# FFN weight tiles of an attention and FFN kernel: transposed by DMA from SBUF instead of by TensorE

## The reference

```
x = x + Wo(softmax(q k^T) v),  q from layernorm(x), k and v from the context
x = x + FFN(layernorm(x))
FFN: gate = q_act(x) @ q_w(w_gate)^T;  up = q_act(x) @ q_w(w_up)^T
     out  = q_act(silu(gate) * up) @ q_w(w_down)^T
q_w: blocks of 32 share a power-of-two scale; elements are rounded and clipped to +-6 times it
```

## Time and profile before

| | |
|---|---|
| median of 3 runs | 2190.7 us (2190.6 to 2194.46) |
| the profiled execution | 2190.88 us |
| its span, first to last instruction | 2189.3 us |
| outside the span | 1.6 us |
| PE / DVE / ACT / POOL busy | 95% / 70% / 47% / 36% |
| mean granted TensorE clock | 0.986 of full |

### The profile page before, as it was taken

The page is one execution under the profiler, slowest core; times in us unless marked ns, Lnnn a source line. Parts: engine busy times, 40 slices in busy tenths (PEclk is TensorE's granted clock), DMA queues, the critical chain, the costliest instruction groups (busy, mean ns, idle before and its releaser), DMA issues.

```text
span 2189.3 us, 49860 instructions
## 1 busy us (share of the span) xinstructions
PE 2085.6 (95%) x15818; PEld 1535.8 (70%) x15818; DVE 1533.2 (70%) x3455; ACT 1035.8 (47%) x2760; POOL 791.9 (36%) x1093
## 2 busy tenths in 40 slices
PE   6899999999999999999999999999999978999996
PEld 5678777877787877777787877787888853444442
DVE  6777776777777776777676767676665548777774
ACT  7755554555555554545454545455544532333331
POOL 4333333332333333333232323331111006666664
PEclk9999999999999999999999999999999998999998
DMA  6733433232333333333333333232232253544444
GB/s 219 185 79 73 83 69 88 64 78 69 79 73 78 74 76 76 76 76 76 72 76 76 76 76 76 67 74 62 61 63 59 52 152 65 85 82 84 84 84 66
DMA packets 398607, 179.55 MB, mean 82 GB/s; under 512 B 361984, under 2 KB 374784, under 8 KB 398400
## 3 DMA queue, kind: packets, MB, share of 16 engines
q1 hardware_dynamic: 375616, 125.10, 27.7%
q0 software_dynamic: 16608, 45.36, 8.5%
q10 hardware_dynamic: 6176, 6.29, 0.9%
HBM read 61.08 MB, written 27.26 MB: 40 GB/s over the span
## 4 chain that ended last, share of the span: by engine, by line
PE 80%; issue 4%; DVE 4%; DMA 4%; POOL 3%; ACT 3%; SPq 1%; POOLq 0%; DVEq 0%; ACTq 0%
PE b_qk L1019 30%; PE b_v L1019 15%; PE b_o L1074 7%; PE b_c L1019 7%; PE b_s L1019 7%; PE b_w L1074 7%; DMA attn_weights<-x_scratch 2%; POOL attn_weights L514 2%; PE b_pt L1019 1%; DMA probT<-psplit 1%; PE b_x L1019 1%; PE b_w L1162 1%; PE b_x L1026 1%; DVE inner_amax L951 1%; SPq L328 1%
## 5 line engine op out<-in xcount | busy, mean ns | idle before, releaser
L559 ACT ACTIVATE qk<-b_qk 128x512 f16<-128x512 f32 x256 | 152.7, 596 | 663.6 <-PE b_s L1019 663.5
L857 DVE TENSOR_REDUCE nmax<-b_s 128x2 f32<-128x512 f32 x257 | 177.7, 691 | 371.9 <-PE b_s L1019 371.9
L1019 PE MATMUL b_qk<-xT,attn_weights 128*128 (+1 forms) x3072 | 382.8, 275 | 25.6 <-issue 23.8
L1019 PE MATMUL b_v<-attn_weights,kvT 128*128 128x256 f16 x3072 | 377.2, 273 | 8.0 <-POOL attn_weights L390 8.0
L1019 PE MATMUL b_qk<-kvT,attn_weights 128*128 (+1 forms) x3072 | 384.6, 276 | 0.0
L1019 PEld LDWEIGHTS b_qk<-xT,attn_weights 128*128 128x128 f16 x3072 | 301.6, 99 | 66.2 <-issue 26.9
L881 DVE SCALAR_TENSOR_TENSOR psplit<-prob,rrec,psplit 128x256 f16<-128x256 f32 x514 | 287.1, 600 | 80.5 <-ACT psplit L600 80.5
L1019 PEld LDWEIGHTS b_qk<-kvT,attn_weights 128*128 128x128 f16 x3072 | 304.4, 99 | 38.5
L1019 PEld LDWEIGHTS b_v<-attn_weights,kvT 128*128 (+1 forms) x3072 | 300.2, 98 | 43.8 <-issue 9.0
L600 ACT ACTIVATE psplit<-prob,rrec 128x256 f16<-128x256 f32 x514 | 233.0, 500 | 95.9 <-DVE rrec L874 95.6
L590 ACT ACTIVATE prob<-b_s,nmax 128x256 f32<-128x256 f32 x514 | 238.8, 469 | 33.3 <-DVE nmax L857 1.6
(11 more groups left out here) (124 smaller groups left out, 2736.7 us busy)
## 6 DMA issues: line engine op xcount, KB each, us to landing
ffn_w<-wffn SPq DMA_DIRECT2D x48, 256.0 KB, 3.2
acc<-xtok POOLq DMA_DIRECT2D x16, 512.0 KB, 4.0
out<-acc POOLq DMA_DIRECT2D x16, 512.0 KB, 4.3
out<-attn_weights POOLq DMA_DIRECT2D x32, 256.0 KB, 4.1
xrow<-xq POOLq DMA_DIRECT2D x61, 128.0 KB, 3.7
kvrow<-kvt POOLq DMA_DIRECT2D x61, 128.0 KB, 3.3
stage<-wattn SPq DMA_DIRECT2D x12, 512.0 KB, 3.8
ffn_scratch<-ffn_t SPq DMA_DIRECT2D x48, 128.0 KB, 1.8
```

The costliest lines, as they stand in the source:

```text
L559: eng.activation(dst, src, ACT.Copy, scale=scale).then_inc(sm[done], 1)
L857: eng.tensor_reduce(nmax[:, :], bS[:, :].rearrange("p (q f) -> p q f", q=2), AX_X, ALU.max, negate=True).then_inc(sm["max_done"], 1)
L1019: last = eng.matmul(out, l, r, start=(a == 0), stop=(a == len(pairs) - 1))
```

## The change

PE's transposes and ACT's copy go. SP issues a DMA transpose from `wb` to `wt` behind the probabilities of head 2, and stores `wt` behind those of head 3, not head 0. `ffn_moved` now counts the DMA's 16 and also gives POOL its permit to write `wb` again; `ffn_tr` is gone.

```diff
             def store_ffn(w):
-                eng.wait_ge(sm["ffn_moved"], w + 1)
+                eng.wait_ge(sm["ffn_moved"], 16 * (w + 1))
...
+            def transpose_ffn(w):
+
+                wait_apart(eng, "ffn_q", w + 1)
+                if not isinstance(w, int) or w > 0:
+                    wait_apart(eng, "ffn_stored", 16 * w)
+                eng.dma_start_transpose(wt[:, :].rearrange("p (c f) -> p c f", c=4), wb[:, :]
+                                        ).then_inc(sm["ffn_moved"], 16)
...
             def ffn_quad(n, store=True, load=True):
                 for k in range(QUAD):
                     transpose_p(4 * n + k, k % 2)
-                    if store and k == 0:
+                    if store and k == 2:
+                        transpose_ffn(n - FFN_FROM - 1)
+                    if store and k == 3:
                         store_ffn(n - FFN_FROM - 1)
...
 (POOL, round_ffn)
-                eng.wait_ge(sm["ffn_tr"], w)
+                eng.wait_ge(sm["ffn_moved"], 16 * w)
                 eng.tensor_tensor(by_block(wb[:, :]), by_block(wr), spread(ws), ALU.mult).then_inc(sm["ffn_q"], 1)
...
 (ACT, quad)
-                    if ffn and k == 0:
-                        w = n - FFN_FROM - 1
-                        eng.wait_ge(sm["ffn_tr"], w + 1)
-                        if not isinstance(w, int) or w > 0:
-                            eng.wait_ge(sm["ffn_stored"], 16 * w)
-                        eng.activation(wt[:, :], pW, ACT.Copy).then_inc(sm["ffn_moved"], 1)
...
 (PE, quad_at)
-                    if ffn and k == 0:
-
-                        w = n - FFN_FROM - 1
-                        eng.wait_ge(sm["ffn_q"], w + 1)
-                        if not isinstance(w, int) or w > 0:
-                            eng.wait_ge(sm["ffn_moved"], w)
-                        for c in range(4):
-                            last = eng.transpose(pW[:, c * P:(c + 1) * P], wb[:, c * P:(c + 1) * P], identb[:, :])
-                        last.then_inc(sm["ffn_tr"], 1)
```

More of the change, by code:

```diff
@@ L167, in build @@
                                             ("b_s", "b_qk", "b_c", "b_v", "b_pt", "b_o", "b_x", "b_w")]
-        pW = bPT[:, 0:256].bitcast(BF16)
         o_bank = [bO, bW]
@@ L183, in build @@
             ffn_loaded ffn_amax ffn_pow ffn_scale ffn_inv ffn_y ffn_exp ffn_magic ffn_add ffn_sub ffn_clip ffn_q
-            ffn_tr ffn_moved ffn_stored gate_up_resident down_resident
+            ffn_moved ffn_stored gate_up_resident down_resident
             t_stats t_aggr t_step t_rstd t_xn x_amax_done x_pow_done x_scale_done x_inv_done x_round x_clip x_q
```

## The result

| | before | after |
|---|---|---|
| median of 4 runs each, on one chip | 2191.86 us (2190.6 to 2194.46) | 2234.04 us (2229.23 to 2236.42) |
| ratio, 95% interval | | 1.0188 (1.0166 to 1.021) |
| the profiled execution, its span | 2190.88, 2189.3 us | 2236.22, 2234.7 us |
| mean granted TensorE clock | 0.986 | 0.977 |

The changed kernel is slower by 1.9%; the span grew by 45.4 us where the forecast took 16 off.

What follows compares the result with a forecast made beforehand. PE's own work was taken to bound the tile stretch, other engines having slack. From 2190.9 us, 11.0 for transposes and 5.0 for fewer low-clock returns came off, with new delays priced at 0: 2174.9 us, range 2168 to 2187.

Steps and rivals of the forecast that it cites:

- What is dealt again: PE's loop returns: they fall elsewhere in time, low-clock ones go from six to three of ten, 5.0 us less.
- its pause isn't longer: PE's loop returns: the pause, 2.4 us each, was taken not to grow, one reason to expect fewer low-clock returns.
- 23.8 us that nothing releases: PE's idle time over 1270 us of the tile stretch: ten pauses, read as the returns of its loop.
- Transposes at 0.23 us a tile: PE, head 0: removing four transposes per tile saves 0.23 us, 48 times, 11.0 us in all.
- Rival 3: PE's transposes cost their full durations, 42 us in all, giving 2149 us; chance 0.02.
- the estimate of 52.8 us: PE's transposes at the skill's 275 ns each: 1.1 us a tile, giving 2138 us.
- ACT's copies: ACT loses 48 copies of 0.58 us, 27.8 us in all, outside the quad's chain: worth nothing.
- rival 1: SP's queue: the new DMA delays head 2's probT; at 1.5 us of delay, 2208.7 us; chance 0.05.
- 0.4 us or more is left: Slack before PE wants head 3's probabilities, even landing 1.0 to 1.5 us later; so the DVE collision costs 0.
- rival 2: Head 0: the transposes' time returns as a wait for probT or the context's low half; 2190.9 us, chance 0.06.
- three returns at the lower level: PE's clock behind loop returns: three of ten low instead of six, 3 x 1.67 = 5.0 us less, a judgement.
- any deal of the clock: Low-clock returns anywhere from none to ten: from 2179.9 us, 2169.9 to 2186.6; chance 0.87 for this case.

Runs made afterwards that it cites:

- e1: The changed kernel with 35 idle increments at the head of PE's program: 2184.47 us, 0.9968 of before.
- e2: The kernel before the change with 221 idle increments at the head of PE's program: 2265.95 us, 1.0333 of before.
- e4: The changed kernel with 35 idle increments at the head of PE's program and two buffers of ffn_b: 2178.73 us, 0.9938 of before.
- e6: The kernel before the change with 55 idle increments at the head of PE's program: 2213.65 us, 1.0096 of before.
- e10: The changed kernel with 129 idle increments, putting the loop's jump back 26 instructions behind a block's edge: 2207.26 us in one timed execution.
- e3: The changed kernel with 16 idle increments at the head of PE's program: 2189.08 us, 0.9983 of before.
- e5: The changed kernel with two buffers of ffn_b and 53 idle increments, where e4 has 35: 2183.92 us, 0.9971 of before.
- e8: The changed kernel with 178 idle increments, putting the loop's first instruction 90 ahead of a block's end: 2191.84 us in one timed execution.

## Why the prediction was wrong

1. **The step that failed is "What is dealt again".** It let the returns fall elsewhere in time and dealt the clock again, but took the return itself as fixed ("its pause isn't longer"). The pause of a return depends on where the loop's code lies, and a change that takes 35 + 39 instructions off PE moves it. The sum had no term for it: +29.6 us of pauses, +16 of clock behind them, and a part of the 6.9 of waits. None of the rivals was this one; its row was there, as 23.8 us that nothing releases. The shown cause: e1 undoes only the place and gets 50 us back, e2 does only the place and loses as much.
2. **Transposes at 0.23 us a tile: right.** Head 0 went to 6.53 and the quad down by 0.22 us. Rival 3 is out: by it head 0 would have become 0.875 us shorter (42 / 48). So is the estimate of 52.8 us from the Trainium skill ("TensorE: Matmul & The Clock Gate", Part 4: PE-mode transpose). ACT's copies cost nothing, as said.
3. **The DMA transpose: nearly right.** Predicted landing 2.6 us (2.5 to 3.0); measured a median of 2.4, just under that range, with 4.7 at most, in the view of the tile (DMA to landing):

```profile
L285 SPq DMA_TRANSPOSE ffn_t<-ffn_b x48: 1188/1189/1190, 184.8 to 1526.6; - x48
DMA to landing us min/median/max: 1.7/2.4/4.7
```

It doesn't delay the `probT` ahead of it in the queue: head 2's lands after 3.26 us at most, 3.05 at the median (370 to 1440 us), and rival 1 didn't happen.
4. **POOL and DVE: the delays right, one DMA left out.** Line 425 waits 3.69 us for the DMA, 3.4 having been expected, and line 884 of head 3 is held up, 1.29 us and in every fourth quad 2.10, for 0.88. POOL's timeline and DVE's, after:

```profile
1013.77 1.05 POOL L425 TENSOR_TENSOR ffn_b<-ffn_magic_rounded,ffn_scale 128x512 bf16<-128x512 f32 x1 [3.69 <-DMA ffn_t<-ffn_b]
```

```profile
1014.20 1.29 DVE L884 SCALAR_TENSOR_TENSOR psplit<-prob,rrec,psplit 128x256 f16<-128x256 f32 x2 [0.30 <-ACT psplit L609]
...
1040.84 2.10 DVE L884 SCALAR_TENSOR_TENSOR psplit<-prob,rrec,psplit 128x256 f16<-128x256 f32 x2 [0.30 <-ACT psplit L609]
```

The probabilities of head 3 are late by 0.41 and 1.22 us, where 0.3 and 1.0 were expected. "0.4 us or more is left" holds as long as they land in 3.0 us. In every fourth quad they land after 4.5 to 5.2 us, and the slack is gone: POOL's store of `x_scratch`, which stands behind line 443 and which the prediction didn't follow, now falls 0.3 us behind their issue, and a block fetch comes on top. That 3.0 us wasn't sure could be read before the change: head 3's probabilities in the quads with n % 4 = 0, where PE comes to them only 8 us or more behind their issue because its loop returns in between, landed after 3.86 to 5.24 us, 4.79 on average. PE's timeline after the change at a quad that waits, and the DMA view of it:

```profile
1047.80 0.83 PE L1022 MATMUL b_c<-probT,vbuf 128*128 128x256 f16 x6 [0.64 <-DMA probT<-psplit]
```

```profile
q8 instruction: 1, 0.02, 2.1%
...
x_scratch<-x_quantised POOLq DMA_DIRECT2D x1, 128.0 KB, 4.1
...
probT<-psplit SPq DMA_TRANSPOSE x1, 4.7
```

This is a small rival 2, reached by a way that it didn't name. Double buffering (e4) gave 5.7 us for it against e1, of which 3.4 are waits of `b_c`; the rest may be the clock (two low-clock returns for four).
5. **The clock: not as taken.** The forecast chose three returns at the lower level; there were ten, each after a return with two pauses. With one long pause there were ten (e6) and seven (e10). In kernels with one short pause there were one to six, and no run tells what decides those, so this stays open. Executions of one kernel differ by up to 11 us (e3: 2184.27 to 2194.94), as much as the gain sought.
6. **With the code at its old place the time falls into the forecast's range, at its upper end.** e1 is that: 2184.47 us, against 2174.9 forecast and 2179.9 before any deal of the clock. Against its own comparison (2192.86 us) it gained 8.4 us, where the forecast took 16 off. The 5.0 us of `b_c` waits are the largest part of the difference, and a fourth low-clock return another 1.7; the rest is not attributed. With two buffers and 44 increments the forecast's number is met, 2173.93 us, but that is another kernel, with one low-clock return where the forecast took three.

## What to carry to other kernels

An edit that adds or removes instructions of an engine with a loop moves the loop against the blocks in which its code is fetched, here PE's (no other engine's loop was tried): count the engine's instructions ahead of the loop and in it before and after, and look at the pauses named "issue" at each return before looking for another cause. If a change that shortens PE makes the kernel slower, pad its program's head with idle instructions, at a place where the engine waits anyway, until the pair of pauses is one: here 35 increments were worth 50 us. A transposed operand should have more slack than its landing time in a quiet queue suggests; here they landed 1.3 us later at the median when a block was fetched beside them, up to 3.0 later, and 0.9 later when POOL's store was issued right behind them. When a change delays an engine, follow its DMA issues too, and look at what they will meet.

## What the runs showed of the hardware that was not expected

- A return of PE's loop costs 2.1 to 2.8 us. If the loop's first instruction has only 12 or 30 instructions ahead of a 256-instruction edge, a second pause follows, 2.4 to 3.6 us or 1.84 us on average; with 90 there is none. If the jump back lies 26 instructions behind an edge, the pause is 3.0 to 4.5 us. The 256 is worked out from the 12 and 30 instructions between the pauses with 238 increments between them, and agrees with after and with before plus 221 increments.
- A DMA transpose that is in flight when an instruction block is fetched lands late. The thirteen traces have 2493 transposes into `probT` between 170 and 1500 us. With a fetch of PE's code beginning 0.7 to 2.3 us behind the issue, and none of the other instruction queue near, 147 landed after 3.45 to 6.09 us, median 4.36. With no fetch of either queue from 0.5 us ahead to 3.5 us behind, 1693 had a median of 3.05; 1663 of these landed by 3.26, and the other 30 (3.84 to 4.03) are the ones with POOL's store of `x_scratch` issued within 1 us behind them. That the fetch is a cause is shown by e5, where the fetches alone were moved and the late transposes moved with them; for the store it rests on this count and on e8 and e10; how either holds the transpose up is not shown.
- An idle increment at the head of PE's program costs about 0.15 us once the engine has no wait left to hide it (the first matmul at 20.87, 28.37, 35.11 and 37.78 us with 129, 178, 221 and 238 of them).
- DVE's line 884 was held up by the two-input operation of POOL that runs beside it (1.29 and 2.10 us for 0.88). The Trainium skill, "SBUF — State Buffer", section SBUF: two separate sides, states a lock of the shared port pair for whole instructions, and the trace agrees: the part of line 884 that meets line 425 ends 0.28 us behind it (1015.10 after 1014.82), and the one that meets line 452 the same 0.28 behind that (1042.94 after 1042.66).
